# Moving a tile's LayerNorm tail from the head to the end of the feed-forward loop body

## The reference, cut to what is computed

```python
# x: (8, 4096, 1024) float32, one batch row per core
x = x + _layernorm(linear_attn(_layernorm(x), W_qkv, W_o))
x = x + _layernorm(ffn(_layernorm(x), w1, b1, w2, b2, gamma, beta))

def ffn(x):                                  # hidden = 4096
    h = layernorm(x) * gamma + beta
    h = qlinear(h, w1, b1)                   # 8-bit values by row, ternary weights
    h = gelu(h)
    return qlinear(h, w2, b2)
def qlinear(x, w, b):
    xq, sx = act_quant(x)                    # scale = 127 / max|x| of the row
    wq, sw = weight_quant(w)
    return xq @ wq.T / (sx * sw) + b
```

## Time and profile before

| | |
|---|---|
| median of 3 runs | 3614.93 us (3611.18 to 3618.12) |
| the profiled execution | 3607.72 us |
| its span, slowest core (core 1) | 3606.2 us |
| spans of the eight cores | 3573.9 to 3606.2 us |
| PE busy | 2087.3 us (58%) |
| DVE busy | 1538.9 us (43%) |
| ACT busy | 723.7 us (20%) |
| mean granted TensorE clock, core 1 | 0.776 |

### The profile page before, as it was taken

One profiled execution on the slowest core, in us unless ns is written; L12 is line 12 of the kernel. 1 busy time (PEld: TensorE's weight loads), 2 busy tenths in 40 slices (PEclk: granted clock), 3 DMA queues, 4 the chain that ended last, 5 costly groups with the idle time before them and its releaser, 6 DMA issues.

```text
span 3606.2 us, 33891 instructions; the slowest of 8 cores (3573.9 to 3606.2 us)
## 1 busy us (share of the span) xinstructions
PE 2087.3 (58%) x10640; PEld 1032.4 (29%) x10640; DVE 1538.9 (43%) x2492; ACT 723.7 (20%) x1193; POOL 147.6 (4%) x203
## 2 busy tenths in 40 slices
PE   0151567746667367646766376746676366656665
PEld 0041434412222144312222143412222244322222
DVE  0576543354543143444553134354452143455442
ACT  0030321112222021222221022122221121122221
POOL 0141300000000000000000000000000000000000
PEclk9999576768888666768878677678887676687887
DMA  9897901131210411130121311031012311122101
GB/s 187 243 196 237 177 21 33 24 108 27 41 40 22 131 27 27 27 111 21 41 41 32 123 27 27 24 111 41 21 41 38 120 26 34 38 88 41 41 21 44
DMA packets 333137, 245.50 MB, mean 68 GB/s; under 512 B 304272, under 2 KB 304288, under 8 KB 328864
## 3 DMA queue, kind: packets, MB, share of 16 engines
q0 software_dynamic: 97440, 184.58, 18.7%
q1 hardware_dynamic: 235520, 58.74, 8.8%
HBM read 159.41 MB, written 33.55 MB: 54 GB/s over the span
## 4 chain that ended last, share of the span: by engine, by line
PE 38%; DVE 21%; DMA 21%; ACT 9%; issue 7%; DVEq 2%; another core or an unknown queue 0%; SPq 0%; ACTq 0%; POOL 0%; POOLq 0%; PEldq 0%; PEld 0%
PE pb L988 13%; PE pb L906 11%; DMA abf<-abf 6%; PE pb L492 5%; DMA af<-x 5%; DMA af<-w 4%; PE pb L499 3%; DMA w2q_t<-w2qs 3%; PE pb L909 2%; DMA w2qs<-abf 1%; DMA out<-x 1%; DVE af L949 1%; DVE abf L953 1%; DMA wqkv_t<-w_qkv 1%; ACT af L917 1%
## 5 line engine op out<-in xcount | busy, mean ns | idle before, releaser
L906 PE MATMUL pb<-w1q_t,abf 128*128 128x512 fp8e4 x2048 | 546.4, 415 | 487.3 <-DMA abf<-abf 428.1
L988 PE MATMUL pb<-w2q_t,abf 128*128 128x512 fp8e4 x2048 | 477.7, 394 | 78.4 <-ACT s2rowr L977 44.5
L906 PEld LDWEIGHTS pb<-w1q_t,abf 128*128 128x128 bf16 x2048 | 192.1, 104 | 767.0 <-issue 613.7
L492 PE MATMUL pb<-abf,wqkv_t 128*128 128x128 bf16 x2048 | 192.2, 284 | 253.9 <-DMA abf<-abf 253.9
L988 PEld LDWEIGHTS pb<-w2q_t,abf 128*128 128x128 bf16 x2048 | 201.4, 101 | 337.1 <-issue 124.8
L492 PEld LDWEIGHTS pb<-abf,wqkv_t 128*128 128x128 bf16 x2048 | 187.6, 133 | 257.8 <-issue 257.8
L1012 DVE BATCH_NORM_STATS2 bns<-af 128x6 f32<-128x512 f32 x32 | 22.2, 695 | 524.0 <-ACT af L1003 524.0
L921 DVE TENSOR_REDUCE khs<-af 128x1 f32<-128x1024 f32 x128 | 156.2, 1220 | 173.8 <-ACT af L917 105.0
L528 DVE TENSOR_REDUCE khs<-pb 128x8 f32<-128x512 f32 x32 | 22.1, 692 | 439.4 <-ACT af L509 439.4
L917 ACT ACTIVATE af<-pb,scal 128x512 f32<-128x512 f32 x256 | 160.4, 684 | 233.3 <-PE pb L909 223.6
L294 DVE TENSOR_REDUCE af<-af 128x1 f32<-128x4096 f32 x16 | 70.7, 4420 | 150.9 <-DMA af<-w 150.9
(11 more groups left out here) (162 smaller groups left out, 2741.7 us busy)
## 6 DMA issues: line engine op xcount, KB each, us to landing
af<-w POOLq DMA_DIRECT2D x16, 2048.0 KB, 10.1
wqkv_t<-qkvs POOLq DMA_DIRECT2D x3, 6144.0 KB, 22.9
af<-w POOLq DMA_DIRECT2D x32, 512.0 KB, 5.3
af<-w POOLq DMA_DIRECT2D x16, 1024.0 KB, 9.9
af<-x POOLq DMA_DIRECT2D x32, 512.0 KB, 4.0
w1q_t<-w1qs POOLq DMA_DIRECT2D x4, 4096.0 KB, 16.0
w2q_t<-w2qs POOLq DMA_DIRECT2D x4, 4096.0 KB, 25.2
out<-x POOLq DMA_DIRECT2D x32, 512.0 KB, 2.9
```

The costliest lines, as they stand in the source:

```text
L492: mi = PE.matmul(pq, lhsT=wqkv[:, kk, m * 128:(m + 1) * 128], rhs=hf[:, kk, :], start=(kk == 0), stop=(kk == 7))
L906: PE.matmul(Bk[bb0 + n2][:, :], lhsT=xf[:, kk, :], rhs=w1q[:, kk, hs0:hs0 + 512], start=(kk == 0), stop=False)
L988: mi = PE.matmul(Bk[4 + n2][:, :], lhsT=xq2_fm[:, kk, :], rhs=w2q[:, kk, n2 * 512:n2 * 512 + 512], start=(kk == 0), stop=False)
```

## The change

The call of `f_tail(gg - 1)` moves from the head of the body of the FFN loop to its end, behind `f_f2(gg)`. The functions are unchanged, and so are their instructions and the number of them. On every engine, the instructions of the tail of tile gg-1 now stand behind those of `f_front_tp(gg+1)`, `f_q2(gg)`, `f_front(gg+2)`, `f_f1(gg+1)` and `f_f2(gg)`, and the last iteration issues the tails of tiles 6 and 7 one behind the other.

```diff
         f_f1(0)
         for gg in range(G):
-            if gg >= 1:
-                f_tail(gg - 1)
             if gg + 1 < G:
                 f_front_tp(gg + 1)
             f_q2(gg)
@@ -1054,6 +1052,8 @@
             if gg + 1 < G:
                 f_f1(gg + 1)
             f_f2(gg)
+            if gg >= 1:
+                f_tail(gg - 1)
         f_tail(G - 1)
         ms[f"pe_ffn_done_{seg}"] = cnt["pe"]
```

## The result

| | before | after |
|---|---|---|
| median | 3615.69 us (3608.21 to 3623.27, 8 runs) | 3532.06 us (3522.87 to 3539.06, 8 runs) |
| ratio | | 0.9769, 95% interval 0.9754 to 0.9783 |
| the profiled execution | 3607.72 us | 3539.06 us |
| spans of the eight cores | 3573.9 to 3606.2 us | 3493.7 to 3537.5 us |

By the medians the change makes the kernel 83.6 us faster. Forecast were 3510 us and a range of 3490 to 3556; the measured 3532.06 lies inside the range, 22 us above the 3510. The profiled execution of the kernel before was faster than each of its eight runs, and that of the changed kernel is the slowest of its eight, so the two stand only 69 us apart. The parts are therefore compared by pieces inside the traces, not by the spans.

A forecast was written before the change was run, and what follows sets the result against it. Bound: the chain z, square root, normalization, addition, store, transpose, f_f1, kept by ACT's order. 4 x (17.1 + 11.7 - 3.6) = 100.8 us off gives 3506.9 to 3514.1, forecast 3510 us, range 3490 to 3556.

The forecast's parts named there:

- The naive reading: Tail wholly hidden in every interval, each shrinking to 35.4 us; 464 us saved, about 3146; chance 0.03.
- A: Gap between f_f2(0) and f_f1(2) goes, as iteration 1 opens without tail(0); saves 17.1 us per segment, bounds 15.5 and 18.5.
- B: From z(1) to z(7), DVE's tail statistics run during f_f2 and leave the chain; saves 1.95 us six times, 11.7 per segment.
- The link of the chain: On ACT, the square root's table load starts 0.03 us after z instead of 1.98 later; saves 1.95 us a tile.
- all move forward together: Store, f_q2 and f_front start from the same addition, so nothing else becomes due and the 1.95 us is saved.
- C: Two tails in a row after z(7) at each segment's end; 3.6 us per segment lost, on the path.
- The table load behind a wide z: Rival: the load starts later behind the 512-wide z, taking at most all 1.95 us; 3554 to 3561; chance 0.09.
- stall on the GELU in f_f1(2): Slab 2 of f_f1(2) may start at 1660.0, slab 1 ends 1660.3: no stall, 0.3 us to spare; otherwise a sign of error.
- The rival on the clock: Half clock in f_f1(2) and f_f2(1) of the new dense stretch: 27.6 us lost per segment, about 3620; chance 0.03.
- The third level: Peak-current limit taking a die to 13/16 clock once three cores run dense matmuls; loss smaller than at half clock.

The follow-up runs named there:

- the fillers in both kernels: 6 unused matmuls between the second row of scales and the wait for s2rowr, added to the kernel before (3585.65 us) and to the changed kernel (3492.08 us).
- one_gap_less: Kernel before, with only tail(0) moved behind f_f2(1), later tails still at the head of the iteration; 3557.18 us, ratio 0.9871.
- stats_late: Changed kernel plus a wait, so DVE takes the statistics of tail(gg-1) only once z(gg) is out of PSUM; 3568.61 us, ratio 0.9900.
- filler_in_gap: Changed kernel plus 6 unused 512-column matmuls between turning the second row of scales and the wait for s2rowr; 3492.08 us, ratio 0.9688.
- no_double_tail: Changed kernel with tail(6) issued ahead of f_f2(7), so only one tail follows z(7); 3525.33 us, ratio 0.9786.
- the tail in the shadow: Changed kernel with f_f2 cut in two, tail(gg-1) issued between the second row of scales and f_f2's matmuls; 3165.57 us, ratio 0.8757.

## Why the prediction was right, and what it mis-sized

**What bounds the loop: right.** The naive reading, that the tail leaves the gap, would have given about 3146 by the prediction's own rival. The tail's square root stands behind z(gg) on ACT, so the gap stayed for another tile's data. The kernel with the tail ahead of z(gg) shows it from the other side: against the changed kernel only the tail's place ahead of f_f2's matmuls and z differs, the gap is gone, and 0.876 of the time before is left.

**A: right in mechanism, mis-sized by 1.3 us.** 17.1 us per segment were forecast, 15.8 measured (53.0 to 37.2). The step that failed is "the second row of scales at 1668.9, f_f2(1) 1.76 us later, and z(1) 14.81 us after that", which gives f_f2(1) the length of f_f2(0), 10.52 us for its 48 matmuls. In every segment on every core it had 12.21 us. By that alone the miss would be 1.7 us; it is smaller because the first interval of the kernel before was 53.0 us on the mean, and not the 52.5 that the prediction took as the middle of two. With the fillers in both kernels A is 16.3 us (51.9 to 35.6).

**B: right in mechanism, mis-sized by 4.1 us.** 11.7 us per segment were forecast, 7.6 measured (5 x 1.26 + 1.3). The link of the chain is 1.95 us as forecast (2.06 by the gap, 1.97 with the clock held). The step that failed is "all move forward together": the instructions did, but f_f2 fell into its long form more often. On core 4, 10 of the 28 f_f2 of tiles 0 to 6 had the long form before, and 21 of 28 after (9 to 11 and 21 to 22 on every core); eleven times 1.69 us is 4.6 us per segment, and the last tile's 48 matmuls went from 12.2 to 12.9. That is 5.4 us, as much as the forecast 28.8 of A and B together lies above the measured 23.4. That the two agree so closely is in part luck, since clock pieces outside f_f2 move too; but with f_f2 held in its short form on both sides, A and B together are 27.9 to 28.5 us. The matmuls of L988 show it on the page as well: 477.7 us busy before, 497.8 after.

**C: right**, 3.5 against 3.6 us, four times, and on the path each time: 3.53 us in the last segment, and about 3.4 us, on the mean of two profiles each, up to the start of the next attention stage.

**The sum**, with the clock's share: 4 x (15.8 + 7.6 - 3.5) = 79.6 us, against 83.6 by the medians; the 4 us left are less than what the stretches between the segments move from one profile to the next (2 to 3 us each).

**The rivals.** The table load behind a wide z took nothing (0.02 us). No stall on the GELU in f_f1(2). The rival on the clock named the right stretch and much too large a price: one dip of 1.69 us in it, not two functions at half level. What rows 8 show holds for both kernels: their four profiles have no granted clock but full and half. The third level that the rival names did come up elsewhere, for some 30 to 80 us on each of four cores in the profiles of one_gap_less, stats_late, filler_in_gap and no_double_tail, and for longer with the tail in the shadow. I had priced half clock only as a disaster on the other side and left it out of the sum, though rows 2 had its short and long form side by side.

## What to carry to other kernels

When a function is moved in a program of in-order engines, follow its instructions on each engine and ask what each now stands behind. Here moving the tail behind f_f2 as a whole put its square root behind a copy out of PSUM that waits for PE, and bought one gap of seven; putting it between the two halves of f_f2 bought all seven. The profile's longest wait named a transpose whose removal gave nothing in the intervals where a second path of the same length lay behind it, and 8 us in the one where none did: a mean over unlike intervals would have hidden both. And a price read from one tile at full clock can be too low: where a trace has the same group at two lengths, the sum needs both and how often each comes.

## What the runs showed of the hardware

- With a pause of PE of 1.6 us between dense stretches, the granted clock fell to its half level (0.55 in the two windows behind it) and cost 1.69 us in some tiles, and stayed full in others, at the same length of pause (1.59 and 1.60 us). Shortening the gap ahead by 2 us took the share from 9 to 11 of 28 to 21 or 22 of 28, on every core; what decides for a single tile wasn't found. Six unused matmuls in the pause, leaving 0.30 us idle, took the long form away in all 224 groups of tiles 0 to 6.
- In five of the eleven experiments' profiles cores of one die (0 to 3 or 4 to 7) had stretches at a granted clock of 0.81, of up to 17 us each; with the tail in the shadow, 54 matmuls ran there in the time of 65 at full clock.
- An ACT_TABLE_LOAD can start 0.02 us after a 128x512 activation ends (1668.49 to 1668.51 in the changed kernel).
